# A rotary attention of 16 heads as one pipeline over four passes, with maxima ahead of copies on VectorE

## The chip, the cores and the metric

The kernel runs on 1 core of one Trainium2 chip. The metric is the device time of one execution in microseconds. The kernel before took 2139.44 us as the median of 3 runs (2137.86 to 2139.44).

## The reference

The reference is a chain of eight residual layers over 8 sequences of 256 tokens of width 128, all in fp32. Each layer adds `f(layernorm(x))` to `x`. The fifth is the layer that the change rewrites:

```
Q, K, V = x @ W_Q.T, x @ W_K.T, x @ W_V.T        # 16 heads of 8
Q, K = rope(Q), rope(K)                          # x * cos + flipped(x) * sin
scores = Q K^T / sqrt(8), causal mask
out = softmax(scores) V
return out.reshape(B, S, 128) @ W_O.T
```

Before it stand a linear attention, a feed-forward with 8 experts, a wide attention (16 heads of 64) and the same feed-forward; behind it a feed-forward with 32 experts, a state-space layer and that feed-forward again.

## The kernel before

The 2048 tokens are four passes of T = 512 (two sequences of L = 256). The residual `x` stays in SBUF, channels on partitions. The layers run one after another, each in a block of its own, which ends when all its engines have ended. Most layers are already one block over all four passes. The rotary attention is not: `attend` (L1939) calls `rotary_attention` (L325) once for each pass, so it is four blocks. Behind them `cut_weights` (L293) is a block that splits the up weights of the next layer into a high and a low part, ScalarE the high (L308) and VectorE the low (L314); these weights are loaded by a DMA issued just before the layer (L1931).

A pass has an edge at its start: the norm (L195 to L221: centre on TensorE, Square, mean, Ln and Exp on ScalarE, the product on VectorE), four projections into four banks (L369: query, its flipped form, key, its flipped form), the values (L371), 12 products that only keep TensorE running (L189), the rotation on VectorE (L473 to L475) and four copies of the key, each with all but one head in four set to zero (L477), so that one product over 32 rows gives the scores of one head. GpSimd clears the values' buffer (L440), and ScalarE lays the values into it (L448), 128 columns for each head of which 8 are not zero.

Then come 16 stages. A stage is (sequence b, head c within four, half jj): two heads m = 0, 1, each with 128 queries against 128 keys and 128 queries against 256 keys, that is 384 columns of scores. For a stage:
- TensorE: `scores(i)` (L385, L386) into banks 2(i%2) and 2(i%2)+1; `turn(i)`, six transposes of probabilities (L397) into banks 4 and 5; `weigh(i)`, the products with the values (L417, L419), which accumulate in bank 6. The order is scores(i+2), turn(i+1), weigh(i).
- VectorE: four operations (L491) that add the causal mask (`trib`), write the negated scores to SBUF and take the row minimum; then two copies of transposed probabilities (L501). In its round i it takes the minima of stage i and the copies of stage i-1.
- ScalarE: four exponentials in place with the sum of each row (L456).

scores(i) waits for the minima of stage i-2; turn(i) for the exponentials of stage i and for the copies of stage i-1; weigh(i) for the copies of stage i. Each pass ends with the reciprocals of the sums (L481, L482), their transposes (L405, L461), the product with them (L507), the output projection (L435) and the residual (L509).

Of the kernel before, what the change touches and what calls it, by code (L numbers as in the profile page):

```python
# [6 lines left out]
PASSES = 4  # L7
# [21 lines left out]
WARM = {"first": 4, "squares": 1, "norm": 6, "features": 10, "rotary": 12, "conv": 8, "parts": 24, "residual": 3}  # L29
# [12 lines left out]
def tables():  # L42

    const = layout([("mean", P), ("centre", P), ("ident", P), ("trib", 3 * P), ("cosq", L), ("sinq", L),
                    ("cosk", L), ("sink", L), ("keep", T), ("heads", P), ("hot", 2 * P), ("rows", 4), ("eps", 1),
                    ("seg0", NT * E0), ("seg1", NT * E1)])
    half = layout([("sel0", (E0 + 1) * P), ("sel1", (E1 // 2) * P), ("pick", 16 * P), ("lower", P), ("ones", P),
# [128 lines left out]
NORM = ["n_cent", "n_sq", "n_var", "n_ln", "n_rstd", "n_out"]  # L176

def halves():
    return [slice(b * L, (b + 1) * L) for b in range(NB)]  # L180

# [7 lines left out]

def norm_tensor(k, pe, s, p):

    for n, cols in enumerate(halves()):
        pe.matmul(k.bank[6 + n][:, 0:L], k.c("centre"), k.x[:, p, cols], start=True, stop=True).then_inc(s["n_cent"], 1)  # L195
    keep_clock(k, pe, WARM["squares"])
    for n, cols in enumerate(halves()):
        pe.wait_ge(s["n_sq"], n + 1)
        pe.matmul(k.bank[6 + n][:, L:2 * L], k.c("mean"), k.sq[:, cols], start=True, stop=True).then_inc(s["n_var"], 1)
    keep_clock(k, pe, WARM["norm"])  # L200
    pe.wait_ge(s["n_out"], NB)

def norm_scalar(k, act, s, then):

    for n, cols in enumerate(halves()):
        act.wait_ge(s["n_cent"], n + 1)
        act.activation(k.sq[:, cols], k.bank[6 + n][:, 0:L], ACT.Square).then_inc(s["n_sq"], 1)
    for n, cols in enumerate(halves()):
        act.wait_ge(s["n_var"], n + 1)  # L210
        act.activation(k.sq[:, cols], k.bank[6 + n][:, L:2 * L], ACT.Ln, bias=k.c("eps")).then_inc(s["n_ln"], 1)
        act.wait_ge(s["n_ln"], n + 1)
        act.activation(k.sq[:, cols], k.sq[:, cols], ACT.Exp, scale=-0.5).then_inc(s["n_rstd"], 1)
    if then is not None:
        act.preload_act_table_set(then)

def norm_vector(k, dve, s):
    for n, cols in enumerate(halves()):
        dve.wait_ge(s["n_rstd"], n + 1)  # L220
        dve.tensor_tensor(k.xn[:, 0, cols], k.bank[6 + n][:, 0:L], k.sq[:, cols], ALU.mult).then_inc(s["n_out"], 1)  # L221
    dve.wait_ge(s["n_out"], NB)
# [68 lines left out]

def cut_weights(k, n):  # L293

    nc = k.nc
    width, step = k.up_at[n][1], 4 * P
    cuts = [slice(at, at + step) for at in range(0, width, step)]
    s = k.semaphores(f"cut{n}", ["high"])
    with nc.Block(no_gpsimd_drain=True) as block:
        @block.sync  # L300
        def _(sp):
            k.zero_stale(sp, s)

        @block.scalar
        def _(act):
            act.wait_ge(k.up_loaded[n], 16)
            for cols in cuts:
                act.activation(k.up_high[n][:, cols], k.up_whole[n][:, cols], ACT.Copy).then_inc(s["high"], 1)  # L308

        @block.vector  # L310
        def _(dve):
            for i, cols in enumerate(cuts):
                dve.wait_ge(s["high"], i + 1)
                dve.tensor_tensor(k.up_low[n][:, cols], k.up_whole[n][:, cols], k.up_high[n][:, cols].bitcast(F32),  # L314
                                  ALU.subtract)

ATTEND = NORM + [
          "proj", "low", "high", "qk", "vcopy", "dve", "scores", "probs_in", "probs", "turned", "pt", "pv",
          "sums", "prod", "cleared", "k_turned", "k_tokens", "state", "states", "wide", "wide_t", "ot", "y",  # L320
          "done", "v", "v_act", "v_dve", "q", "qc", "q_low", "k", "kc", "k_low", "max", "pt_act", "pt_dve",
          "outn", "ot_act", "ot_dve"]

def rotary_attention(k, n, p):  # L325

    nc = k.nc
    G, layer, tag = 3, "rot", f"{n}p{p}"
    s = k.semaphores(f"attend{p % 2}", ATTEND)
    w = lambda name: k.w(G, name)
    stages = [(b, c, jj) for b in range(NB) for c in range(4) for jj in range(2)]
    NS = len(stages)
    with ExitStack() as ctx:  # L340
        def sb(name, shape, dt=F32):
            return ctx.enter_context(nc.sbuf_tensor(f"{layer}_{name}{tag}", shape, dt))
        vm = sb("v_by_head", [P, NT, H * (P + DA)])
        by_head = vm[:, :, 0:H * (P + DA)].rearrange("p t (h x) -> p t h x", x=P + DA)[:, :, :, 0:DA]
        q, kk = sb("q", [P, T]), sb("k", [P, T])
        km = sb("km", [P, 4, T])
        t1, t2 = sb("t1", [P, T]), sb("t2", [P, T])
        pin = sb("pin", [P, 2, 2, 3 * P])
        pt = sb("pt", [P, 2, 2, 3 * P])
        low = sb("low", [P, 2, 4])  # L350
        den = sb("den", [P, NT, H])
        wide = sb("wide", [P, NT, H, DA])
        ot = sb("ot", [P, T])
        block = ctx.enter_context(nc.Block(no_gpsimd_drain=True))

        @block.sync
        def _(sp):
            k.zero_stale(sp, s)

        @block.tensor  # L360
        def _(pe):
            pe.wait_ge(k.loaded, 16)
            pe.wait_ge(k.half_loaded, 16)
            pe.wait_ge(k.w_loaded[G], 16)
            norm_tensor(k, pe, s, p)

            names = ["wq", "wqf", "wk", "wkf"]
            for n, name in enumerate(names):
                pe.matmul(k.bank[n][:], w(name), k.xn[:, 0, :], start=True, stop=True).then_inc(s["proj"], 1)  # L369
            for j in range(NT):  # L370
                ins = pe.matmul(k.bank[4][:, j * P:(j + 1) * P], k.xn[:, 0, j * P:(j + 1) * P], w("wv"),  # L371
                                start=True, stop=True)
            ins.then_inc(s["proj"], 1)
            keep_clock(k, pe, WARM["rotary"])

            def scores(i):
                b, c, jj = stages[i]
                pe.wait_ge(s["qk"], c + 1)
                if i >= 2:
                    pe.wait_ge(s["probs_in"], i - 1)  # L380
                for m in range(2):
                    j = 2 * jj + m
                    r = slice(32 * j, 32 * j + 32)
                    t0, o = b * L, k.bank[2 * (i % 2) + m]
                    pe.matmul(o[:, 0:P], q[r, t0:t0 + P], km[r, c, t0:t0 + P], start=True, stop=True)  # L385
                    ins = pe.matmul(o[:, P:P + L], q[r, t0 + P:t0 + L], km[r, c, t0:t0 + L],  # L386
                                    start=True, stop=True)
                ins.then_inc(s["scores"], 1)

            def turn(i):  # L390

                pe.wait_ge(s["probs"], i + 1)
                if i >= 1:
                    pe.wait_ge(s["pt"], i)
                for m in range(2):
                    for n in range(3):
                        ins = pe.transpose(k.bank[4 + m][:, n * P:(n + 1) * P],  # L397
                                           pin[:, i % 2, m, n * P:(n + 1) * P], k.c("ident"))
                ins.then_inc(s["turned"], 1)

            def turn_shares():

                pe.wait_ge(s["wide"], 1)
                for j in range(NT):
                    ins = pe.transpose(k.bank[7][:, j * P:(j + 1) * P],  # L405
                                       wide[:, j].rearrange("p h e -> p (h e)"), k.c("ident"))
                ins.then_inc(s["wide_t"], 1)

            def weigh(i):

                b, c, jj = stages[i]
                pe.wait_ge(s["pt"], i + 1)
                for m in range(2):
                    head = 4 * (2 * jj + m) + c
                    p, first, last = pt[:, i % 2, m, :], c == jj == m == 0, head == 4 * 3 + 3
                    v = lambda tile: vm[:, tile, head * P:(head + 1) * P]
                    pe.matmul(k.bank[6][:, b * L:(b + 1) * L], v(2 * b), p[:, 0:L], start=first, stop=False,  # L417
                              skip_group_check=True)
                    ins = pe.matmul(k.bank[6][:, b * L + P:(b + 1) * L], v(2 * b + 1), p[:, L:L + P],  # L419
                                    start=False, stop=last, skip_group_check=True)  # L420
                ins.then_inc(s["pv"], 1)
# [1678 lines left out]
```

## Time and profile before

| what | us |
|---|---|
| median of 3 runs | 2139.44 (2137.86 to 2139.44) |
| profiled execution | 2135.41 |
| its span | 2133.6 |
| rotary attention, four passes | 879.0 to 1166.2 |
| cut of the next weights | 1166.2 to 1172.4 |
| busy over the whole span: PE, DVE, ACT, POOL | 1862.2, 1563.9, 879.9, 686.1 |
| mean granted TensorE clock | 0.968 |

### The profile page before, as it was taken

Reading aid. Unit: us, or ns where it says so; the run is one execution under the profiler, and the core shown is the slowest. Engines: PE = TensorE matmul, PEld = TensorE weight load, DVE = VectorE, ACT = ScalarE, POOL = GpSimd, SP = SyncE. Lnnn points to the kernel's source line nnn. Section 1 sums busy time; section 2 is a strip of 40 time slices with the busy share of each in tenths; the row PEclk is TensorE's granted clock in tenths of the full one; section 3 lists DMA queues with packets and bytes.
Section 4 is the critical chain, followed back from the end, with each engine's and each line's share of the span. In section 5 each row is a group of like instructions: output and inputs, shape, how many; then the busy total and the mean of one; then the engine's idle time right before and its main releaser. Section 6 shows DMA issues by size and latency. Waiting matters only on the chain. (4 is left out here: it accounts for less than half of the span.)

```text
span 2133.6 us, 23947 instructions
## 1 busy us (share of the span) xinstructions
PE 1862.2 (87%) x7515; PEld 996.0 (47%) x7527; DVE 1563.9 (73%) x2933; ACT 879.9 (41%) x2055; POOL 686.1 (32%) x757
## 2 busy tenths in 40 slices
PE   5779998999997999899888899968888878878998
PEld 2336653555553555567666455523232322225555
DVE  4868884555553788656556688749999999978887
ACT  2125544554543445345445333245444353332232
POOL 2642322433432222210110000027767677750000
PEclk8999999999999899999999899979999999999999
DMA  5000000000000000100000000000000000000000
GB/s 230 1 0 1 1 1 1 1 1 1 1 1 1 1 1 1 40 1 1 1 1 1 1 1 1 0 15 1 15 1 15 1 1 15 1 0 0 1 1 20
DMA packets 9628, 20.10 MB, mean 9 GB/s; under 512 B 1056, under 2 KB 8224, under 8 KB 8608
## 3 DMA queue, kind: packets, MB, share of 16 engines
q1 hardware_dynamic: 9504, 18.59, 2.6%
q8 instruction: 61, 1.00, 0.2%
q14 instruction: 63, 0.52, 0.1%
HBM read 14.39 MB, written 1.05 MB: 7 GB/s over the span
## 5 line engine op out<-in xcount | busy, mean ns | idle before, releaser
L1816 POOL TENSOR_TENSOR ssm_hc<-ssm_h,ssm_cm 128x512 f32<-128x512 f32 x256 | 334.3, 1308 | 135.3 <-DVE ssm_h L1899 135.0
L1899 DVE TENSOR_TENSOR_SCAN ssm_h<-banks,ssm_dbx 128x512 f32<-128x512 f32 x256 | 313.9, 1227 | 2.3 <-DVE ssm_dbx L1891 2.3
L515 PE MATMUL banks<-ffn_x_high,up_high 128*128 128x512 f32 x544 | 288.8, 531 | 6.0 <-ACT ffn_s1g L992 2.6
L1700 PE MATMUL banks<-ssm_hc,const 128*128 128x512 f32 x512 | 266.1, 601 | 12.2 <-DVE ssm_gated L1874 9.3
L1791 ACT ACTIVATE banks<-banks,a_neg 128x510 f32<-128x510 f32 x256 | 167.2, 659 | 242.6 <-PE banks L1687 241.6
L516 PE MATMUL banks<-ffn_x_low,up_high 128*128 128x512 f32 x544 | 218.3, 401 | 0.0
L517 PE MATMUL banks<-ffn_x_high,up_low 128*128 128x512 f32 x544 | 218.3, 401 | 0.0
L550 POOL TENSOR_TENSOR x_norm<-x_centred,x_square 128x512 f32<-128x512 f32 x28 | 37.9, 1354 | 492.5 <-ACT x_square L545 492.0
L1510 ACT ACTIVATE ffn_th<-banks 128x512 f32<-128x512 f32 (+1 forms) x136 | 81.2, 597 | 273.3 <-PE banks L517 224.6
L1891 DVE TENSOR_TENSOR ssm_dbx<-banks,ssm_bm 128x512 f32<-128x512 f32 x256 | 174.9, 683 | 19.3 <-PE banks L1690 18.8
L1325 POOL TENSOR_SCALAR wide_pin<-wide_pin,wide_rden 128x256 f32<-128x256 f32 x256 | 117.6, 478 | 217.0 <-DVE wide_rden L1349 217.0
L1687 PE MATMUL banks<-ssm_packed,half 96*128 96x510 bf16 x256 | 101.3, 396 | 73.2 <-DVE ssm_h L1899 66.1
L1460 PE MATMUL banks<-ffn_a,weights 128*128 128x512 f32 (+1 forms) x272 | 143.4, 608 | 22.6 <-DVE ffn_a L1550 21.8
L456 ACT ACTIVATE rot_pin4p<-rot_pin4p,rot_low4p 128x128 f32<-128x128 f32 (+1 forms) x256 | 113.1, 443 | 98.9 <-DVE rot_low4p L491 98.9
L1687 PEld LDWEIGHTS banks<-ssm_packed,half 96*128 96x128 bf16 x256 | 25.0, 98 | 261.3 <-DVE ssm_h L1899 235.7
L515 PEld LDWEIGHTS banks<-ffn_x_high,up_high 128*128 128x128 f32 x544 | 104.2, 192 | 86.3 <-issue 38.8
L1532 DVE SCALAR_TENSOR_TENSOR ffn_p<-ffn_th,banks 128x512 f32<-128x512 f32 (+1 forms) x136 | 93.2, 685 | 64.8 <-ACT ffn_th L1510 63.9
L516 PEld LDWEIGHTS banks<-ffn_x_low,up_high 128*128 128x128 f32 x544 | 104.7, 192 | 54.4 <-issue 38.9
L1700 PEld LDWEIGHTS banks<-ssm_hc,const 128*128 128x128 f32 x512 | 98.0, 193 | 56.1 <-POOL ssm_hc L1816 20.0
L1043 POOL TENSOR_SCALAR ffn_hg<-ffn_hg 128x512 f32<-128x512 f32 x72 | 44.2, 613 | 238.9 <-DVE ffn_hg L1063 238.9
L1302 ACT ACTIVATE wide_pin<-banks,wide_low 128x256 f32<-128x256 f32 x256 | 117.4, 477 | 8.0 <-DVE wide_low L1365 8.0
L491 DVE CUSTOM_DVE_ANT_0 rot_pin4p<-banks,const 128x128 f32<-128x128 f32 (+1 forms) x256 | 75.9, 354 | 58.5 <-PE banks L386 58.5
(245 smaller groups left out, 3623.5 us busy)
## 6 DMA issues: line engine op xcount, KB each, us to landing
ssm_packed<-ssm_parts SPq DMA_DIRECT2D x48, 64.0 KB, 2.0
up_whole<-in_up SPq DMA_DIRECT2D x1, 2304.0 KB, 16.2
weights<-in_weights SPq DMA_DIRECT2D x1, 2048.0 KB, 21.4
up_whole<-in_up SPq DMA_DIRECT2D x1, 2048.0 KB, 7.9
const<-in_const SPq DMA_DIRECT2D x1, 1426.5 KB, 6.2
half<-in_half SPq DMA_DIRECT2D x1, 1408.0 KB, 9.7
weights<-in_weights SPq DMA_DIRECT2D x1, 1168.0 KB, 23.9
weights<-in_weights SPq DMA_DIRECT2D x1, 1152.0 KB, 11.2
```

Of the source, the lines that this page charges most:

```text
L515: pe.matmul(out, w_high, x_high, start=True, stop=False)
L516: pe.matmul(out, w_high, x_low, start=False, stop=False)
L517: return pe.matmul(out, w_low, x_high, start=False, stop=True)
L1302: ins = act.activation(pin[:, i % RING, m, cols], k.bank[2 * (i % 2) + m][:, cols], ACT.Exp, bias=low[:, i % RING, n:n + 1], accum_out=den ...
L1325: ins = pool.tensor_scalar(part, part, rden[:, i % RING, n:n + 1], 1.0, ALU.mult, ALU.mult)
L1460: pe.matmul(k.bank[5][:], w("sd" if n == 0 else f"d{n - 1}")[0:rows, :], a[0:rows, g % 2, :], start=(n == 0), stop=(n == N - 1)).then_inc( ...
L1687: pe.matmul(two(k.bank[DELTA[i % AHEAD]])[:, :, 1:], pick, two(packed[0:96, p % 2, 0, g, :])[:, :, 1:], start=True, stop=True) \
L1700: pe.matmul(k.bank[5][:], k.c("hot")[:, P - row:2 * P - row], hc[:, i % HOLD, :], start=(i % NP == 0), stop=(i % NP == NP - 1)).then_inc(s ...
L1791: act.activation(spot_i, spot_i, ACT.Exp, scale=k.a_neg[:, i % NP:i % NP + 1]).then_inc(s["da"], 1)
L1816: pool.tensor_tensor(hc[:, i % HOLD, :], h[:, i % HOLD, :], cm[:, i // NP % 2, :], ALU.mult) \
L1891: dve.tensor_tensor(dbx[:, i % AHEAD, :], k.bank[DELTA_X[i % AHEAD]][:], bm[:, i // NP % 2, :], ALU.mult) \
L1899: dve.tensor_tensor_scan(h[:, n % HOLD, :], k.bank[DELTA[n % AHEAD]][:], dbx[:, n % AHEAD, :], 0.0, ALU.mult, ALU.add).then_inc(s["h"], 1)
```

## The change

`rotary_attention` becomes one block over the 64 stages of all four passes.

- The norm, the projections and the rotation of pass p+1 are issued within the stages of pass p (`ahead`, slots 6 to 13). All of them use bank 7. For pass 0 they run before the first stage.
- TensorE adds the causal mask: four bf16 products of `identb` with a new table `hide` (0 or -1e30), 128 columns each, behind the scores of a stage. The two heads' scores are issued in turns.
- VectorE takes maxima with two reductions over two banks at once, of 2 x 128 and 2 x 256 elements for each row. ScalarE reads the scores from PSUM and writes its exponentials to SBUF, into three buffers.
- The values take 32 columns for each head, so weighing puts the two heads into two column tiles of 32, in turns.
- The sums of the rotation, the four masked keys, the widening of the reciprocals and both parts of the cut of the next weights go to GpSimd, the cut as two of its eight pieces in each pass. The block `cut_weights` is gone, and with it `norm_tensor`, `norm_scalar`, `norm_vector`; `prepare_tensor`, `prepare_scalar`, `prepare_gpsimd` (L523 to L550, used by the other layers) take their place.
- The order on TensorE is scores(i), turn(i-2), weigh(i-3). In its round i VectorE takes the maxima of stage i and then the copies of stage i-3.

The core of the new function (p, b, c, jj = stage(i); NS = 16, ALL = 64, RING = DEEP = 3):

```diff
+        def _(pe):
+            def ahead(p, n):
+                ...
+                if n == 6:
+                    if p >= 1:
+                        pe.wait_ge(s["vm"], p)
+                    if p >= 2:
+                        pe.wait_ge(s["done"], p - 1)
+                    prepare_tensor(k, pe, s, p, 0)
+                if n == 7:
+                    prepare_tensor(k, pe, s, p, 1)
+                if 9 <= n < 13:
+                    c = n - 9
+                    pe.wait_ge(s["n_out"], p + 1)
+                    if c:
+                        pe.wait_ge(s["roped"], 4 * p + c)
+                    pe.matmul(k.bank[7][:], w(("wq", "wqf", "wk", "wkf")[c]), k.xn[:, p % 2, :], start=True, stop=True) \
+                        .then_inc(s["proj"], 1)
+                if n == 13:
+                    ...
+            def scores(i):
+                p, b, c, jj = stage(i)
+                if i % NS == 0:
+                    pe.wait_ge(s["q"], p + 1)
+                pe.wait_ge(s["km"], 4 * p + c + 1)
+                if i >= 2:
+                    pe.wait_ge(s["probs"], i - 1)
+                t0 = b * L
+                for t, (queries, keys) in enumerate(((slice(t0, t0 + P), slice(t0, t0 + P)),
+                                                     (slice(t0 + P, t0 + L), slice(t0, t0 + L)))):
+                    for m in range(2):
+                        r = slice(64 * jj + 32 * m, 64 * jj + 32 * m + 32)
+                        pe.matmul(k.bank[2 * (i % 2) + m][:, tiles[t]], q[r, p % 2, queries], km[r, p % 2, c, keys],
+                                  start=(t == 0), stop=False, skip_group_check=True)
+                for m in range(2):
+                    for first in (0, 2 * P):
+                        ins = pe.matmul(k.bank[2 * (i % 2) + m][:, first:first + P], k.h("identb"), k.h("hide"),
+                                        start=False, stop=True, skip_group_check=True)
+                ins.then_inc(s["scores"], 1)
+            def turn(i):
+                pe.wait_ge(s["probs"], i + 1)
+                if i >= 1:
+                    pe.wait_ge(s["pt"], i)
+                for m in range(2):
+                    for n in range(3):
+                        ins = pe.transpose(k.bank[4 + m][:, n * P:(n + 1) * P],
+                                           pin[:, i % RING, m, n * P:(n + 1) * P], k.c("ident"))
+                ins.then_inc(s["turned"], 1)
+            def weigh(i):
+                p, b, c, jj = stage(i)
+                pe.wait_ge(s["pt"], i + 1)
+                pe.wait_ge(s["vm"], p + 1)
+                if i % NS == 0 and p >= 1:
+                    pe.wait_ge(s["ot"], p)
+                for tile, (queries, part) in enumerate(((slice(b * L, (b + 1) * L), slice(0, L)),
+                                                        (slice(b * L + P, (b + 1) * L), slice(L, L + P)))):
+                    for m in range(2):
+                        j = 2 * jj + m
+                        ins = pe.matmul(k.bank[6][32 * j:32 * j + 32, queries], vm[:, p % 2, 2 * b + tile, 4 * j + c, :],
+                                        pt[:, i % 2, m, part], start=(c == tile == 0), stop=(c == 3 and tile == 1),
+                                        skip_group_check=True)
+                ins.then_inc(s["pv"], 1)
+            ...
+            for n in range(NS):
+                ahead(0, n)
+                if n in (6, 7, 12, 13):
+                    keep_clock(k, pe, WARM["first"])
+            for i in range(ALL + DEEP):
+                p, slot = i // NS, i % NS
+                if i < ALL:
+                    scores(i)
+                if slot == 2 and p >= 1:
+                    turn_shares(p - 1)
+                if slot == 4 and p >= 1:
+                    output(p - 1)
+                if i < ALL:
+                    ahead(p + 1, slot)
+                if 2 <= i < ALL + 2:
+                    turn(i - 2)
+                if i >= DEEP:
+                    weigh(i - DEEP)
+            output(PASSES - 1)
+            ...
+        def _(act):
+            ...
+            for i in range(ALL):
+                p, b, c, jj = stage(i)
+                act.wait_ge(s["max"], i + 1)
+                if i >= RING:
+                    act.wait_ge(s["turned"], i - RING + 1)
+                ...
+                        ins = act.activation(pin[:, i % RING, m, tiles[t]], k.bank[2 * (i % 2) + m][:, tiles[t]], ACT.Exp,
+                                             bias=low[:, i % RING, t, m:m + 1],
+                                             accum_out=den[:, p % 2, 2 * b + t, head:head + 1])
+                ins.then_inc(s["probs"], 1)
+                if i % NS == 2 and p >= 1:
+                    shared(p - 1)
+                ahead(p + 1, i % NS)
+            shared(PASSES - 1)
+        def _(pool):
+            pool.memset(vm[:], 0.0).then_inc(s["cleared"], 1)
+            pool.wait_ge(k.up_loaded[1], 16)
+            ...
+            for p in range(PASSES):
+                prepare_gpsimd(k, pool, s, p)
+                pool.wait_ge(s["roped"], 4 * p + 2)
+                pool.tensor_tensor(q[:, p % 2, :], t1[:], t2[:], ALU.add).then_inc(s["q"], 1)
+                pool.wait_ge(s["roped"], 4 * p + 4)
+                pool.tensor_tensor(kk[:], t1[:], t2[:], ALU.add).then_inc(s["k"], 1)
+                pool.wait_ge(s["k"], p + 1)
+                for c in range(4):
+                    pool.tensor_scalar(km[:, p % 2, c, :], kk[:], k.c("rows")[:, c:c + 1], 1.0, ALU.mult, ALU.mult) \
+                        .then_inc(s["km"], 1)
+                if p >= 1:
+                    widen(p - 1)
+                for i in (2 * p, 2 * p + 1):
+                    cols = cuts[i]
+                    pool.tensor_copy(k.up_high[1][:, cols], k.up_whole[1][:, cols]).then_inc(s["up_high"], 1)
+                    pool.wait_ge(s["up_high"], i + 1)
+                    pool.tensor_tensor(k.up_low[1][:, cols], k.up_whole[1][:, cols],
+                                       k.up_high[1][:, cols].bitcast(F32), ALU.subtract).then_inc(s["up_low"], 1)
+            widen(PASSES - 1)
+        def _(dve):
+            ...
+            for i in range(ALL + DEEP):
+                p, slot = i // NS, i % NS
+                if p >= 1 and slot == DEEP and i < ALL:
+                    normalise(p - 1)
+                if p >= 1 and slot == 5:
+                    residual(p - 1)
+                if i < ALL:
+                    dve.wait_ge(s["scores"], i + 1)
+                    for t in range(2):
+                        ins = dve.tensor_reduce(low[:, i % RING, t, :], k.banks[:, 2 * (i % 2):2 * (i % 2) + 2, tiles[t]],
+                                                AX_X, ALU.max, negate=True)
+                    ins.then_inc(s["max"], 1)
+                if i >= DEEP:
+                    n = i - DEEP
+                    dve.wait_ge(s["turned"], n + 1)
+                    if n >= 2:
+                        dve.wait_ge(s["pv"], n - 1)
+                    for m in range(2):
+                        ins = dve.tensor_copy(pt[:, n % 2, m, :], k.bank[4 + m][:, 0:3 * P])
+                    ins.then_inc(s["pt"], 1)
+                if p >= 1 and slot == 1:
+                    invert(p - 1)
+                if i < ALL:
+                    ahead(p + 1, slot)
+            normalise(PASSES - 1)
+            residual(PASSES - 1)
...
-                cut_weights(k, 1)
...
 PLAN = [linear_attention, biased_ffn, wide_attention, biased_ffn,
-        attend(rotary_attention), capped_ffn, state_space, capped_ffn]
+        rotary_attention, capped_ffn, state_space, capped_ffn]
```

`ahead` on VectorE (slots 9 to 12) multiplies one projection in bank 7 with its table, behind the copies of the round; on ScalarE it is the Square, Copy, Ln and Exp of the norm (slots 6 and 7) and four copies of values (slot 13).

## Rows read from the trace of the kernel before

**Rows 1.** Stretches: us; busy us of PE, PEld, DVE, ACT, POOL; clock; DMA; GB/s.
```profile
879.00:951.00 72.00, 63.50 (x403) 47.25 (x404) 43.22 (x176) 33.30 (x136) 7.35 (x2) 0.95 0.09 30
```

**Rows 2.** The page's costliest groups of instructions, the rotary stages.
```profile
L456 ACT ACTIVATE rot_pin4p<-rot_pin4p,rot_low4p 128x128 f32<-128x128 f32 (+1 forms) x256 | 113.1, 443 | 98.9 <-DVE rot_low4p L491 98.9
...
L491 DVE CUSTOM_DVE_ANT_0 rot_pin4p<-banks,const 128x128 f32<-128x128 f32 (+1 forms) x256 | 75.9, 354 | 58.5 <-PE banks L386 58.5
```

**Rows 3.** The timeline, steady stages: start us, us, instruction [idle before <-releaser].
```profile
907.91 0.50 PE L385 MATMUL banks<-rot_km4p,rot_q4p 32*128 32x128 f32 x4
...
908.78 0.87 PE L397 MATMUL banks<-const,rot_pin4p 128*128 128x128 f32 x6
...
908.90 0.29 DVE L491 CUSTOM_DVE_ANT_0 rot_pin4p<-banks,const 128x128 f32<-128x128 f32 x1 [1.14 <-PE banks L386]
...
909.49 0.60 PE L417 MATMUL banks<-rot_pt4p,rot_v_by_head4p 128*128 128x256 f32 x2
...
910.02 1.02 DVE L501 COPY rot_pt4p<-banks 128x384 f32<-128x384 f32 x2
...
910.89 0.50 PE L385 MATMUL banks<-rot_km4p,rot_q4p 32*128 32x128 f32 x4
...
914.17 0.50 PE L385 MATMUL banks<-rot_km4p,rot_q4p 32*128 32x128 f32 x4
```

**Rows 4.** The timeline, an early stage at the low clock.
```profile
896.20 0.81 PE L385 MATMUL banks<-rot_km4p,rot_q4p 32*128 32x128 f32 x4
...
897.79 1.54 PE L397 MATMUL banks<-const,rot_pin4p 128*128 128x128 f32 x6
...
897.92 0.29 DVE L491 CUSTOM_DVE_ANT_0 rot_pin4p<-banks,const 128x128 f32<-128x128 f32 x1 [0.58 <-PE banks L386]
...
899.12 1.06 PE L417 MATMUL banks<-rot_pt4p,rot_v_by_head4p 128*128 128x256 f32 x2
...
901.66 0.50 PE L385 MATMUL banks<-rot_km4p,rot_q4p 32*128 32x128 f32 x4
```

**Rows 5.** Groups by shape, and the timeline, for kinds of work that are added.
```profile
L1365 DVE TENSOR_REDUCE wide_low<-banks 128x4 f32<-128x1024 f32 x64 | 76.6, 1197 | 6.9 <-PE banks L1202 6.9
...
L619 DVE TENSOR_REDUCE ffn_r_top<-banks 128x4 f32<-128x128 f32 x8 | 2.3, 286 | 0.0
...
503.97 1.08 PE L1228 MATMUL banks<-wide_pt,wide_va 128*64 128x256 f32 x8
...
887.85 2.75 PE L189 MATMUL banks<-half 128*128 128x512 bf16 x12
```

**Rows 6.** The timeline at the stage's ends, groups on GpSimd, DMA issues.
```profile
883.42 3.70 PE L369 MATMUL banks<-x_norm,weights 128*128 128x512 f32 x8 [0.56 <-DVE x_norm L221]
...
885.52 0.69 DVE L473 TENSOR_TENSOR rot_t14p<-banks,const 128x512 f32<-128x512 f32 x1 [2.15 <-PE banks L369]
...
891.52 0.29 DVE L491 CUSTOM_DVE_ANT_0 rot_pin4p<-banks,const 128x128 f32<-128x128 f32 x1
...
1165.24 0.69 DVE L509 TENSOR_TENSOR x_resid<-x_resid,banks 128x512 f32<-128x512 f32 x1 [1.22 <-PE banks L435]
...
1172.40 2.05 PE L526 MATMUL banks<-x_resid,const 128*128 128x512 f32 x2 [6.55 <-PEq L299]
...
L550 POOL TENSOR_TENSOR x_norm<-x_centred,x_square 128x512 f32<-128x512 f32 x28 | 37.9, 1354 | 492.5 <-ACT x_square L545 492.0
...
up_whole<-in_up SPq DMA_DIRECT2D x1, 2048.0 KB, 7.9
```

**Rows 7.** The table of stretches, by granted clock.
```profile
655.66:669.31 13.65, 8.66 (x64) 5.40 (x64) 6.34 (x11) 6.72 (x26) 5.70 (x13) 1.00 0.00 1
669.31:672.73 3.42, 1.43 (x12) 1.12 (x14) 1.29 (x2) 0.00 (x0) 0.56 (x2) 1.00 0.00 0
672.73:679.56 6.83, 6.14 (x14) 2.52 (x11) 0.00 (x0) 0.60 (x1) 0.00 (x0) 0.50 0.00 0
...
1396.36:1410.01 13.65, 10.15 (x16) 2.89 (x14) 4.79 (x8) 7.03 (x9) 0.00 (x0) 0.50 0.01 1
```

More of the change, by code:

```diff
@@ L27 @@
 ALPHA, LIMIT = 1.702, 7.0
-WARM = {"first": 4, "squares": 1, "norm": 6, "features": 10, "rotary": 12, "conv": 8, "parts": 24, "residual": 3}
+WARM = {"first": 4, "features": 10, "parts": 24, "residual": 3}
 BIG = 1e30
@@ L189, in keep_clock @@
         pe.matmul(k.bank[bank][:], k.h("identb"), k.half[:, 0:512], start=True, stop=True)
[L192 to L222, printed above, removed]
 def turn_in(k, x_in):
@@ L290, in _ @@
                 dve.tensor_copy(tok[:, p].rearrange("p j d -> p (j d)"), k.bank[p][:]).then_inc(s["copied"], 1)
[L293 to L315, printed above, removed]
@@ L318 @@
[L318 to L421, printed above, removed]
-            scores(0)
-            scores(1)
-            pe.wait_ge(s["vcopy"], 1)
-            turn(0)
-            for i in range(NS):
-                if i + 2 < NS:
-                    scores(i + 2)
-                if i + 1 < NS:
-                    turn(i + 1)
-                weigh(i)
-            turn_shares()
-            pe.wait_ge(s["ot"], 1)
-            pe.matmul(k.bank[0][:], w("wo"), ot[:], start=True, stop=True).then_inc(s["y"], 1)
-            keep_clock(k, pe, WARM["residual"], bank=3)
-        @block.gpsimd
-        def _(pool):
-            pool.memset(vm[:], 0.0).then_inc(s["cleared"], 1)
-        @block.scalar
-        def _(act):
-            act.wait_ge(k.loaded, 16)
-            norm_scalar(k, act, s, None)
-            act.wait_ge(s["cleared"], 1)
-            act.wait_ge(s["proj"], 5)
-            act.activation(by_head, k.bank[4][:].rearrange("p (t h e) -> p t h e", t=NT, h=H),
-                           ACT.Copy).then_inc(s["vcopy"], 1)
-            for i in range(NS):
-                b, c, jj = stages[i]
-                act.wait_ge(s["probs_in"], i + 1)
-                for m in range(2):
-                    for t, cols in enumerate((slice(0, P), slice(P, 3 * P))):
-                        head = 4 * (2 * jj + m) + c
-                        ins = act.activation(pin[:, i % 2, m, cols], pin[:, i % 2, m, cols], ACT.Exp,
-                                             bias=low[:, i % 2, 2 * m + t:2 * m + t + 1], scale=-1.0,
-                                             accum_out=den[:, 2 * b + t, head:head + 1])
-                ins.then_inc(s["probs"], 1)
-            act.wait_ge(s["wide_t"], 1)
-            act.activation(t2[:], k.bank[7][:], ACT.Copy).then_inc(s["wide_t"], 1)
-        @block.vector
-        def _(dve):
-            link = chained(dve, s["dve"])
-            dve.wait_ge(k.loaded, 16)
-            norm_vector(k, dve, s)
-            rope = [(q, 0, 1, "cosq", "sinq"), (kk, 2, 3, "cosk", "sink")]
-            for o, a, f, cos, sin in rope:
-                dve.wait_ge(s["proj"], f + 1)
-                table = lambda name: spread(k.c(name), [P, NB, L], 1)
-                two = lambda ap: ap.rearrange("p (b t) -> p b t", b=NB)
-                link(dve.tensor_tensor(two(t1[:]), two(k.bank[a][:]), table(cos), ALU.mult))
-                link(dve.tensor_tensor(two(t2[:]), two(k.bank[f][:]), table(sin), ALU.mult))
-                link(dve.tensor_tensor(o[:], t1[:], t2[:], ALU.add))
-            for c in range(4):
-                dve.tensor_scalar(km[:, c, :], kk[:], k.c("rows")[:, c:c + 1], None, ALU.mult).then_inc(s["qk"], 1)
-            def shares():
-                link(dve.reciprocal(den[:], den[:]))
-                dve.tensor_copy(wide[:], spread(den[:], [P, NT, H, DA], 3)).then_inc(s["wide"], 1)
-            for i in range(NS + 1):
-                if i < NS:
-                    dve.wait_ge(s["scores"], i + 1)
-                    if i >= 2:
-                        dve.wait_ge(s["turned"], i - 1)
-                    for m in range(2):
-                        for t, cols in enumerate((slice(0, P), slice(P, 3 * P))):
-                            ins = dve.tensor_tensor_reduce(
-                                pin[:, i % 2, m, cols], k.bank[2 * (i % 2) + m][:, cols],
-                                k.c("trib")[:, cols], 1.0, 3e38, ALU.add, ALU.min,
-                                low[:, i % 2, 2 * m + t:2 * m + t + 1])
-                    ins.then_inc(s["probs_in"], 1)
-                if i >= 1:
-                    dve.wait_ge(s["turned"], i)
-                    if i >= 3:
-                        dve.wait_ge(s["pv"], i - 2)
-                    for m in range(2):
-                        ins = dve.tensor_copy(pt[:, (i - 1) % 2, m, :], k.bank[4 + m][:, 0:3 * P])
-                    ins.then_inc(s["pt"], 1)
-            dve.wait_ge(s["probs"], NS)
-            shares()
-            dve.wait_ge(s["pv"], NS)
-            dve.wait_ge(s["wide_t"], 2)
-            dve.tensor_tensor(ot[:], k.bank[6][:], t2[:], ALU.mult).then_inc(s["ot"], 1)
-            dve.wait_ge(s["y"], 1)
-            dve.tensor_tensor(k.x[:, p, :], k.x[:, p, :], k.bank[0][:], ALU.add).then_inc(s["done"], 1)
@@ L1972 @@
     put(const, const_at[0], "ident", np.eye(P))
-    hide = np.where(tri.T, 0.0, BIG)
-    put(const, const_at[0], "trib", np.concatenate([hide, hide * 0, hide], 1))
     pair = (idx % DA) % (DA // 2)
@@ L2014 @@
     put(half, half_at[0], "lower", tri)
+    put(half, half_at[0], "hide", np.where(tri.T, 0.0, -BIG))
     put(half, half_at[0], "ones", 1.0)
```

131 lines of the change are left out of this document (120 added, 11 removed).

## The prediction

> **What bounds the kernel now.** I read the page first, then the table of stretches for the part that is rewritten. The rotary stage runs from 879.0 us to the start of the next stage's products at 1172.4 [rows 6]: 293.4 us of a span of 2133.6. It is four equal passes of 71.8 us and, at its end, 6.4 us for the cut of the next weights. In a pass TensorE is busy 63.5 of 72 us, VectorE 43, ScalarE 33 and GpSimd 7 [rows 1]. The costliest groups say where the idle time of the others lies: ScalarE waits 98.9 us for row minima, VectorE 58.5 us for scores [rows 2]. So TensorE is the nearest to its bound, and in the steady stages (a pass has 16) it goes score products, transposes, weighing with gaps of tenths: from 907.91 to 910.89 is one stage of 2.98 us, and the next takes 3.28 us, so 3.13 us each [rows 3]. The minima (908.90) start when the scores are there, and the copies (910.02) when the minima are done; TensorE has the scores of two stages ahead in hand, so nothing of this chain closes on itself.
> Beside the steady stages a pass has its edges: 12.5 us from its start to its first minimum at 891.52 [rows 6], and a tail. The first stages run at the low clock: products that take 2.98 us a stage later take 5.46 us between 896.20 and 901.66 [rows 4].
>
> **What goes.** The edges of four passes become one prologue and one tail, and the cut (about 6 us on ScalarE and VectorE) goes to GpSimd. The minimum with an added mask becomes one plain maximum over two banks; the mask goes to TensorE. Weighing puts two heads into two column tiles at once. By busy time this is a lighter stage: VectorE some 2 us for maxima and copies, TensorE 0.86 + 0.23 + 0.71 + 0.65 us, ScalarE four exponentials of 0.44 us [rows 2] or 1.8 us, each plus work for the next pass of under half a us per stage. If engines only had to be kept busy, a stage would take about 2.9 us.
>
> **What comes: a closed loop.** That is not how the waits are laid. In round i TensorE issues scores(i), then turn(i-2), then weigh(i-3). turn(i-2) needs banks 4 and 5 free, and waits for the copy of stage i-3. VectorE takes in round i the maxima of stage i first, for which it waits on scores(i), and only then the copy of stage i-3. So the copy, though its transposes have long been ready, stands behind the maxima; turn(i-2) and weigh(i-3) stand behind the copy; and scores(i+1) are queued behind both on TensorE. All of it is in series: scores(i), maxima(i), copy(i-3), turn(i-2), weigh(i-3), scores(i+1). One trip of it is one stage.
>
> Its price at the full clock:
> - scores to maxima. Now 0.99 us from the first product to the first minimum [rows 3]. Four mask products are added: a bf16 product of 512 columns takes 0.229 us in a row of 12 [rows 5], so 128 columns take 0.057, four 0.23; a change of tile shape costs 0.1 (an fp32 product of 512 columns takes two passes of 0.43 us [rows 6], so two heads of 256 + 128 columns stream for 1.30 of the 1.40 us from 909.49 to 910.89, [rows 3]). 1.32 us. The bound above is 1.5, if each product waits for a weight load of 0.1 us.
> - maxima. The reduce of 128 elements takes 0.286 us and that of 1024 takes 1.197 [rows 5], so 1.02 ns per element: 0.42 for 256 and 0.68 for 512. Each next one starts 0.08 early, as two copies of 0.55 take 1.02. 0.94 us.
> - copy, unchanged in shape: 1.02 us [rows 3], and 0.06 us to TensorE.
> - six transposes: 908.78 to 909.49, 0.71 us.
> - weighing. Now 909.49 to 910.89, 1.40 us with the change of shape; 1.30 is streaming. Column tiles in pairs do run together: eight passes of 256 columns take 1.08 us in the wide attention [rows 5], half of what they would take one after another. 0.65, and 0.2 for two changes of shape: 0.85 us. The bound above is 1.5, if pairs of 32 columns don't overlap.
> Sum: 1.32 + 0.94 + 1.02 + 0.06 + 0.71 + 0.85 = **4.90 us** a stage, against 3.13 now.
>
> On the changes of shape: the rows show 0.1 us for one. The Trainium skill, page TensorEngine Tiling (Array Packing), section Key Properties, says that changing the tiling mode drains the TensorE. By that rule the stage, which has three changes where it had two, would pay for one more; the trace has it at a tenth of a us, which is in the sum.
>
> **What is hidden.** Everything of the next pass is issued by TensorE after scores(i), that is while VectorE does maxima and copy (1.96 us): at most 1.1 us of products a slot. VectorE's rotations, residual and shares (0.69 us each, [rows 6]) fall where it waits for transposes, weighing and scores (some 2.9 us). ScalarE has 1.8 us of work in 4.9, so the Square, Copy, Ln, Exp and four value copies fit. GpSimd's share of a pass (three two-operand operations and two subtractions at 1.3 us [rows 6], and seven lighter operations below that, under 16 us) has 78 us. All are costed at nothing, and the closed loop is their cover; if the loop were broken they would cost 0.3 to 0.5 us a stage. The probabilities (1.8 us after the maxima) are needed two rounds later.
>
> **The clock.** At the low level all TensorE terms double. From the slow stage [rows 4]: scores to first minimum 1.72, with 0.55 for the mask 2.27; transposes 1.33; weighing 2.54 less the change, halved, and two changes: 1.42; VectorE as before, 1.96 + 0.06. Sum 7.04, call it **7.0 us**. Which level holds? In the loop TensorE has nothing to do for some 2 us in each stage. In the last stages of the wide attention it was busy 8.66 of 13.65 us and kept the full clock; when the scores ran out it was busy 1.43 of 3.42 us, and the 6.83 us after that were granted half [rows 7]. In the new loop it is busy 2.8 of 4.9 us as such rows count, which lies between, and in the rounds without work ahead the part around the gap looks like the second. Once low, it would be busy 4.8 of 7.0 us, and a stretch with 10.15 of 13.65 us busy ran at the low level throughout [rows 7]. So it should fall and rise. Between never and always I take half of the time at each level: 1 / (0.5/4.9 + 0.5/7.0) = **5.76 us** a stage.
>
> **The ends.** Prologue: the centring, squares and logarithm as now, 5 us; GpSimd waits for the up weights (issued at 878.2, landed 7.9 us later, [rows 6]) and normalises by 887.5; four projections and rotations go through one bank, each 0.85 to 1.7 + 0.2 + 0.75 us, to 896 or 898; key sum and first mask on GpSimd, 2 us; scores. The first maximum is at 900, against 891.52 now. The next three rounds, bound by the exponentials, take 6.5 us: 27.5 from 879.0 to the maxima of stage 3. Then 60 rounds, then three copies with transposes and weighing between them, 8.5 us, and share product, output, residual of 0.69 us and the block's end, 3.7 us [rows 6]. Fixed part 39.7 us.
> Sum: 39.7 + 60 x 5.76 = 385 us, against 293.4: **+92 us**. The profiled execution took 2135.4 us (span 2133.6) and would take 2227; the median of the runs lies 4 us above it, so I say 2231.
>
> **Rivals.**
> A, the clock stays full. For it: the wide attention kept its clock when it was busy 63% of a stretch [rows 7], and the loop is at 58% without its work ahead and above it with that. Then 39.7 + 60 x 4.9 = 334, +40 us: 2180. Chance 0.17.
> B, the clock is low nearly throughout. 39.7 + 60 x 7.0 = 460, +166 us: 2306. The rows for it: stretches three quarters busy that stayed low, and that score products use 32 rows and weighing 32 columns at a time. Chance 0.17. The Trainium skill, page TensorE: Matmul & The Clock Gate, Part 4 (PE-mode transpose), says that transposes don't count as busy in the same way for the clock. By that rule the clock would see 2.1 busy us of 4.9 and B is what happens, 2306; no row here tells it apart, since the stretch of the wide attention that fell had lost its scores and kept its transposes.
> C, faster: the loop isn't closed, because VectorE reaches its copy before TensorE needs it, or the change otherwise isn't in series as I read it. Its place is the wait for banks 4 and 5. It decides from a stage below (293.4 - 39.7) / 60 = 4.23 us; with the engines kept busy, 2.9 us, the sum is 39.7 + 174 = 214, -80 us: 2060. Against it: waits of the code, which leave no other order, and no row here makes one of the terms 0.67 us shorter. Chance 0.04.
> The forecast, mixed clock: 0.62.
>
> **How the numbers follow.** The time is the forecast's. The range goes from rival A to rival B, 2178 to 2306, and takes in the bounds of mask and weighing (0.2 and 0.65 us a stage, at 60 stages 12 and 39 us above the forecast). Within 0.2% (4 us, about what a measurement of this kernel can tell) there is next to nothing: it would need a stage of 4.2 us by chance, 0.01. Faster is C with its slower half left out, 0.04. Slower has the rest, 0.95.
>
> **What would show it.** In the trace of the changed kernel: stages of the rotary part 4.9 us apart or more; VectorE's copies starting right behind its maxima, not after a wait for transposes; TensorE's longest waits being those of transposes for copies (about 2 us, 60 times); VectorE waiting for the mask products of the scores, some 2.9 us a stage less its work ahead; ScalarE idle more than half of the time; granted clock between 0.6 and 0.9 for the part, with several falls in each pass; maxima of 0.42 and 0.68 us; weighing in 0.7 us. The forecast is wrong if copies start before maxima of the same round, if the part takes under 300 us, or if one level of the clock holds throughout, which gives A or B.

## The result, and the profile after

The changed kernel takes 2244.81 us (median of 4 runs, 2243.88 to 2248.45) against 2139.44 before: ratio 1.0501 (95% interval 1.0484 to 1.0517), 105 us slower. It was forecast at 2231 and within 2178 to 2306. The profiled execution took 2243.88 us with a span of 2242.0, 108.4 above the span before. The next layer's first product starts at 1283.26, where it was 1172.40 [rows 6]; so the rotary part with the cut takes 404.3 us instead of 293.4, +110.9, and the three layers behind it give back 2.5.

Three stretches of the part, in the columns of [rows 1]: the pipeline from the maxima of stage 3 to those of stage 63; a part of pass 0 with work ahead in six of its seven stages (slots 7 to 13); and the last pass from slot 2 on, which has no next pass to work for.

```profile
908.30:1269.86 361.56, 262.19 (x1638) 151.64 (x1638) 129.40 (x261) 113.01 (x507) 32.22 (x36) 0.74 0.00 1
...
935.52:970.09 34.57, 25.10 (x200) 14.36 (x199) 16.04 (x33) 13.89 (x62) 6.49 (x7) 1.00 0.00 1
...
1181.20:1269.86 88.66, 63.14 (x344) 36.30 (x342) 26.63 (x54) 22.81 (x105) 0.20 (x1) 0.60 0.00 0
```

VectorE and ScalarE do not have more to do: in 361.6 us VectorE works 129.4 and ScalarE 113.0, about a third of the time each, where in a pass before they worked 43.2 and 33.3 of 72 us [rows 1]. Yet a stage takes 6.03 us in the mean, where one of the steady part before took 3.13. The time is in waits. From the list of waits of the same pipeline (us in total, times, longest):

```profile
ACT rot_pin L1050 <- DVE rot_low L1136: 245.1, 60, 5.5
DVE rot_low L1136 <- PE banks L945: 220.8, 60, 5.2
...
PE banks L956 <- DVE rot_pt L1145: 99.4, 60, 2.1
```

Each occurs 60 times, once a stage: maxima wait for the mask products, exponentials for maxima, and transposes (L956) for the copies (L1145). Before, the third did not exist. One stage at the full clock, in the timeline, answers to [rows 3]:

```profile
940.46 1.02 DVE L1136 TENSOR_REDUCE rot_low<-banks 128x2 f32<-128x256 f32 x2 [2.99 <-PE banks L945]
941.39 1.01 DVE L1145 COPY rot_pt<-banks 128x384 f32<-128x384 f32 x2
...
942.55 0.84 PE L956 MATMUL banks<-const,rot_pin 128*128 128x128 f32 x6 [2.13 <-DVE rot_pt L1145]
...
943.33 0.84 PE L971 MATMUL banks<-rot_pt,rot_v_by_head 128*32 128x256 f32 x8
944.10 0.92 PE L941 MATMUL banks<-rot_km,rot_q 32*128 32x128 f32 x8
944.96 0.40 PE L945 MATMUL banks<-half 128*128 128x128 bf16 x4
...
945.39 1.02 DVE L1136 TENSOR_REDUCE rot_low<-banks 128x2 f32<-128x256 f32 x2 [2.99 <-PE banks L945]
```

Read it as a ring: maxima, copies, transposes, weighing, scores, mask, maxima. Twice in a trip one engine releases the other: the copies release TensorE's transposes, and the mask products release VectorE's maxima. What lies between follows in each engine's order of issue, without a wait, and the trip takes 4.94 us. The same at the low clock answers to [rows 4] and takes 7.19 us:

```profile
1187.90 1.02 DVE L1136 TENSOR_REDUCE rot_low<-banks 128x2 f32<-128x256 f32 x2 [1.42 <-PE banks L945]
1188.84 1.01 DVE L1145 COPY rot_pt<-banks 128x384 f32<-128x384 f32 x2
...
1190.00 1.51 PE L956 MATMUL banks<-const,rot_pin 128*128 128x128 f32 x6 [2.13 <-DVE rot_pt L1145]
...
1191.44 1.50 PE L971 MATMUL banks<-rot_pt,rot_v_by_head 128*32 128x256 f32 x8
1192.87 1.65 PE L941 MATMUL banks<-rot_km,rot_q 32*128 32x128 f32 x8
...
1195.09 1.02 DVE L1136 TENSOR_REDUCE rot_low<-banks 128x2 f32<-128x256 f32 x2 [5.24 <-PE banks L945]
```

### The profile page after: what moved, and what is told of

Its sections match the earlier page's. It is cut to its first block and busy times, and to the rows that moved or that the text cites. A ratio compares the mean times of both kernels' runs of the same rounds, so it can differ in the third digit from the quotient of the medians.

```text
span 2242.0 us, 23945 instructions
## 1 busy us (share of the span) xinstructions
PE 1900.3 (85%) x7698; PEld 976.0 (44%) x7698; DVE 1527.3 (68%) x2505; ACT 865.8 (39%) x2051; POOL 702.9 (31%) x802
## 5 line engine op out<-in xcount | busy, mean ns | idle before, releaser
L1740 PE MATMUL banks<-ssm_hc,const 128*128 128x512 f32 x512 | 266.9, 603 | 12.2 <-DVE ssm_gated L1914 9.3
L1136 DVE TENSOR_REDUCE rot_low<-banks 128x2 f32<-128x256 f32 (+1 forms) x128 | 65.4, 552 | 232.0 <-PE banks L945 232.0
L291 POOL TENSOR_TENSOR x_norm<-x_centred,x_square 128x512 f32<-128x512 f32 x32 | 42.9, 1340 | 528.3 <-ACT x_square L286 524.3
L1050 ACT ACTIVATE rot_pin<-banks,rot_low 128x128 f32<-128x128 f32 (+1 forms) x256 | 104.0, 419 | 253.7 <-DVE rot_low L1136 253.7
L956 PE MATMUL banks<-const,rot_pin 128*128 128x128 f32 x384 | 73.1, 342 | 101.8 <-DVE rot_pt L1145 101.8
## 6 DMA issues: line engine op xcount, KB each, us to landing
weights<-in_weights SPq DMA_DIRECT2D x1, 1168.0 KB, 23.9
```

The costliest lines, as they stand in the source:

```text
L1740: pe.matmul(k.bank[5][:], k.c("hot")[:, P - row:2 * P - row], hc[:, i % HOLD, :], start=(i % NP == 0), stop=(i % NP == NP - 1)).then_inc(s ...
```

## The experiments

**First, the loop with its clock held.** The kernel `e2_fill_gap` adds products that nobody reads. They stand in each round in which TensorE has no other work beside the stages, 37 of the 64. The code is abridged:

```diff
                 if i < ALL:
                     ahead(p + 1, slot)
+                    fill(p, slot)      # in free slots: keep_clock(k, pe, 4, bank=7), behind bank 7's last reader
                 if 2 <= i < ALL + 2:
                     turn(i - 2)
```

> The changed kernel, with four bf16 products of 512 columns that nobody reads put on TensorE between scores(i) and turn(i-2), in every slot that has no work ahead. Closed loop with the clock on top of it (my theory): the products (about 0.9 us) lie in TensorE's 2.1 us of waiting, so they cost nothing, and the clock stays full: every stage takes 4.94 us instead of a mean of 6.03, 60 x 1.09 = 65 us less than the changed kernel, about 2180 us. Rival, the slow stages have another cause than the clock (GpSimd's work, waits on bank 7): the stages without work ahead stay at 6.5 to 7.2 us, about 2245 or more.

Measured: 2180.92 us (2175.61 to 2185.05), ratio to the kernel before 1.0197 (1.0178 to 1.0216). The stretch of its pipeline:

```profile
907.00:1203.33 296.33, 218.95 (x1749) 125.34 (x1770) 129.50 (x261) 113.34 (x508) 32.30 (x36) 1.00 0.00 1
```

In a plain stage of its timeline the products (L182) lie in the gap, and the transposes still wait for the copies behind them, 1.27 us instead of 2.13:

```profile
966.06 1.03 PE L182 MATMUL banks<-half 128*128 128x512 bf16 x4
968.36 0.85 PE L956 MATMUL banks<-const,rot_pin 128*128 128x128 f32 x6 [1.27 <-DVE rot_pt L1165]
```

60 stages take 296.3 us, 4.94 each, all at the full clock. So more work on TensorE made the kernel 64 us faster. Two things follow: what a stage took beyond 4.94 us was the clock's, and 0.9 us of products in a gap cost nothing in the loop.

**Then each side of the loop, on that kernel.** Three edits, each alone: the four mask products left out (the scores are then not masked, so the attention isn't causal); one more reduction on VectorE between maxima and copies; the same one behind the copies. The code is abridged.

```diff
-                for m in range(2):                        # e4_fill_no_mask
-                    for first in (0, 2 * P):
-                        ins = pe.matmul(..., k.h("identb"), k.h("hide"), ...)
...
                     ins.then_inc(s["max"], 1)
+                if i < ALL:                               # e5_fill_extra_between
+                    dve.tensor_reduce(spare[:, i, :], k.const[:, 0:256] as 2 x 128, AX_X, ALU.max)
                 if i >= DEEP:
...
                     ins.then_inc(s["pt"], 1)
+                if i < ALL:                               # e6_fill_extra_behind
+                    dve.tensor_reduce(spare[:, i, :], k.const[:, 0:256] as 2 x 128, AX_X, ALU.max)
```

> As the filled kernel, without the four mask products of a stage (the scores are not masked, so the attention isn't causal). Closed loop: whatever is between the scores and the maxima is paid in full, 0.25 to 0.33 us a stage, 16 to 21 us in 64 stages: about 2161 us if the filled kernel takes 2180. Rival, TensorE has slack in each stage, as it idles for 2 us: no difference.

> As the filled kernel, with one reduction of 256 SBUF elements a row, which nobody reads, on VectorE between the maxima and the copies. Closed loop: paid in full, 0.34 us a stage, +22 us in 64 stages: about 2202 us. Rival, VectorE is under half busy and hides it: no difference.

> As the filled kernel, with the same reduction behind the copies of a round, where VectorE waits for scores for some 3 us. Closed loop: hidden, within 2 us of the filled kernel. Rival, VectorE's total work sets the stage: +22 us, as in the kernel that has it between.

| on the filled kernel | median us | against 2180.92 | a stage at the full clock |
|---|---|---|---|
| no mask products | 2163.51 (2161.61 to 2164.25) | -17.4 | 4.62 |
| reduction between | 2204.77 (2201.84 to 2208.96) | +23.9 | 5.27 |
| reduction behind | 2182.98 (2179.43 to 2186.79) | +2.1 | 4.94 |

The stages are the distances of successive maxima in the traces, where nearly all of them are equal. From the maxima of stage 3 to those of stage 63 the filled kernel took 296.3 us, and the three edits 280.8, 319.5 and 298.0. That is 60 times the difference of a stage, and 3.6, 3.5 and 1.6 us for three, two and one stages in which the clock fell after all. Without the mask products, a stage is 0.32 us shorter, although TensorE idles in each. With 0.33 us more on VectorE it is 0.33 us longer or no longer at all, by where the work stands. The two places in the timelines, first between, then behind:

```profile
1164.03 1.02 DVE L1157 TENSOR_REDUCE rot_low<-banks 128x2 f32<-128x256 f32 x2 [0.48 <-PE banks L946]
1164.97 0.41 DVE L1161 TENSOR_REDUCE rot_spare<-const 128x2 f32<-128x256 f32 x1
1165.30 1.01 DVE L1168 COPY rot_pt<-banks 128x384 f32<-128x384 f32 x2
```

```profile
1162.79 1.02 DVE L1157 TENSOR_REDUCE rot_low<-banks 128x2 f32<-128x256 f32 x2 [2.07 <-PE banks L946]
1163.73 1.01 DVE L1166 COPY rot_pt<-banks 128x384 f32<-128x384 f32 x2
1164.66 0.41 DVE L1169 TENSOR_REDUCE rot_spare<-const 128x2 f32<-128x256 f32 x1
```

The reduction of 0.41 us overlaps the next by 0.08, so it moves the copies by 0.33.

**Then the loop opened, from either side,** on the changed kernel without filling. One edit exchanges VectorE's two halves of a round, the other leaves them and issues the scores earlier on TensorE:

```diff
+                if i >= DEEP:                             # e1_copies_first: copies of stage i-3 first
+                    ...
                 if i < ALL:
                     dve.wait_ge(s["scores"], i + 1)
                     ...
-                if i >= DEEP:
-                    ...
```

```diff
+            scores(0)                                     # e3_scores_early
             for i in range(ALL + DEEP):
                 p, slot = i // NS, i % NS
-                if i < ALL:
-                    scores(i)
+                if i + 1 < ALL:
+                    scores(i + 1)
```

> The changed kernel with one edit: in its round VectorE takes the copies of stage i-3 first and the maxima of stage i second. Closed loop: copy(i-3) no longer waits for scores(i), so a trip of the loop goes over two rounds and TensorE becomes the bound, 1.09 + 0.78 + 0.77 us of scores with mask, transposes and weighing and 0.4 us of work ahead, about 3.0 us a stage; 60 x (6.03 - 3.0) = 180 us less than the changed kernel, about 2065 us, faster than the kernel before. Rival, the loss is the clock's alone: then the swap brings the full clock at best, 4.94 us a stage, 2180 us.

> The changed kernel with VectorE's order left as it is (maxima first) and the loop opened on TensorE: scores(i+1) are issued in round i, ahead of turn(i-2). Closed loop: maxima(i) find their scores done a round earlier, so this opens it as well: about 3.0 us a stage, about 2065 us. Rival, it is VectorE's order as such that costs: then it stays near 2245 us.

> Both edits: copies first and scores a round early. Closed loop: one edit is enough, TensorE stays the bound, so the same as the better of the two within 10 us. Rival, each edit takes away a different part of the wait: the two together gain clearly more than either.

| kernel | median us | ratio to before (95%) |
|---|---|---|
| copies first | 2084.07 (2079.91 to 2090.51) | 0.9746 (0.9726 to 0.9765) |
| scores early | 2080.35 (2069.58 to 2083.78) | 0.9709 (0.9682 to 0.9736) |
| both | 2085.62 (2079.80 to 2092.24) | 0.9751 (0.9729 to 0.9774) |

Either edit turns 5% slower into 2.5 to 3% faster, and both together give no more than one. A plain stage of the kernel with copies first, on TensorE:

```profile
948.94 0.82 PE L956 MATMUL banks<-const,rot_pin 128*128 128x128 f32 x6
949.70 0.84 PE L971 MATMUL banks<-rot_pt,rot_v_by_head 128*32 128x256 f32 x8
950.47 0.92 PE L941 MATMUL banks<-rot_km,rot_q 32*128 32x128 f32 x8
951.33 0.40 PE L945 MATMUL banks<-half 128*128 128x128 bf16 x4
951.56 0.82 PE L956 MATMUL banks<-const,rot_pin 128*128 128x128 f32 x6
```

TensorE waits for nothing there; a stage is 2.62 us, and TensorE is the bound. The expected 3.0 us a stage was too low as a mean: the traces have 3.30 with copies first and 3.18 with early scores, so the kernels came 19 and 15 us above the expected 2065. With both edits it is 3.34, since another wait appears: in every second plain stage the scores wait for the exponentials of two stages before, and that stage takes 3.18 us.

```profile
1091.53 0.92 PE L941 MATMUL banks<-rot_km,rot_q 32*128 32x128 f32 x8 [0.49 <-ACT rot_pin L1051]
```

What is hidden in the closed loop lies bare in the open one. Rounds with work ahead take 3.53 us (2.62 + 0.91), and between slots 2 and 6 the shares product and the residual stand on VectorE ahead of the maxima and wait. That gave a last edit, on the kernel with early scores: the two put behind the maxima of their round. The kernel with early scores ran again beside it, as `e3_again`.

```diff
-                if p >= 1 and slot == DEEP and i < ALL:
-                    normalise(p - 1)
-                if p >= 1 and slot == 5:
-                    residual(p - 1)
                 if i < ALL:
                     ...
                     ins.then_inc(s["max"], 1)
+                if p >= 1 and slot == DEEP and i < ALL:
+                    normalise(p - 1)
+                if p >= 1 and slot == 5:
+                    residual(p - 1)
```

> The kernel with scores a round early, and the shares product (slot 3) and the residual (slot 5) put behind the maxima of their round instead of ahead of them. With the loop open, work that was hidden in it lies on the path: in the trace of the kernel with early scores the maxima of slot 3 stand 2.5 us behind the shares product's wait, and those of slot 5 some 1.9 us behind the residual's. If that is what those rounds lose, three passes gain up to 13 us: about 2068 to 2072 us. Rival, TensorE is the bound there as well and its products of those slots only move: within 3 us of the kernel with early scores, 2080 us.

> The kernel with scores a round early, unchanged, beside it on the same chip: 2080 us as before, to compare the other with.

Measured: 2073.03 us (2068.66 to 2074.46), ratio 0.9690 (0.9677 to 0.9703); beside it early scores alone 2082.35 us (2069.25 to 2083.80), ratio 0.9724 (0.9698 to 0.9749). This is the lowest median, 3.1% under the kernel before. But the two intervals touch, and it isn't shown that the kernel with the edit is faster than the one without: the runs of early scores fall into two groups, near 2069.4 and near 2082, and the lower one is as fast as this. The difference of the groups is for the most part not the attention's: of the 14.2 us between a trace of each (spans 2067.7 and 2081.9), 9.3 lie in the layers before and behind it, whose code is the same. The timelines around slot 3, first early scores alone, then with the edit:

```profile
955.22 1.02 DVE L1137 TENSOR_REDUCE rot_low<-banks 128x2 f32<-128x256 f32 x2 [0.21 <-PE banks L945]
956.15 1.01 DVE L1146 COPY rot_pt<-banks 128x384 f32<-128x384 f32 x2
959.72 0.69 DVE L1120 TENSOR_TENSOR rot_ot<-banks,rot_shares 128x512 f32<-128x512 f32 x1 [2.55 <-PE banks L971]
960.33 1.01 DVE L1137 TENSOR_REDUCE rot_low<-banks 128x2 f32<-128x256 f32 x2
```

```profile
963.00 1.02 DVE L1133 TENSOR_REDUCE rot_low<-banks 128x2 f32<-128x256 f32 x2 [0.67 <-PE banks L945]
964.88 0.69 DVE L1120 TENSOR_TENSOR rot_ot<-banks,rot_shares 128x512 f32<-128x512 f32 x1 [0.86 <-PE banks L971]
```

The wait of 2.55 us before the shares product shrinks to 0.86. From the maxima of slot 2 to those of slot 7 it is 955.22 to 971.70 in the one, and 960.38 to 975.63 in the other: 16.48 and 15.25 us, so 1.2 us a pass and 3.7 in three. That is all that the traces show for the edit. The expected 13 took each wait for a loss; most of them only moved TensorE's products of those slots, as the rival had it. That the median of 2073.03 lies so near the expected 2068 to 2072 is luck.

## Why the prediction was right

**The closed loop** is what happened, and it is shown from six sides: the 60 waits of transposes for copies, the two prices paid in full, the one hidden, and the two openings. Term by term at the full clock, predicted and measured: scores with mask to maxima 1.32 and 1.29 us; maxima 0.94 and 0.93; copies to the first transpose 1.08 and 1.16; transposes 0.71 and 0.78; weighing 0.85 and 0.77. Sum 4.90 and 4.94. At the low clock 7.0 and 7.19. TensorE's terms did not double there, as the prediction put it before it took them from [rows 4]: transposes went from 0.78 to 1.44 us, weighing from 0.77 to 1.43, and all of them together from 2.84 to 5.09. The split of the part before doesn't quite add up either: four passes of 71.8 us leave 6.2 us for the cut, not 6.4; the sum uses only the total.

**Small bounds.** The mask costs 0.32 us in the run without it, against 0.33 in the sum (0.23 and a change of shape of 0.1). The timeline of the kernel with copies first has 0.23 us from the first mask product to the next transposes, which leaves 0.09 us for the change of shape; no run measures it by itself. The Trainium skill, page TensorEngine Tiling (Array Packing), section Key Properties, says that changing the tiling mode drains TensorE. The 0.09 us are what the runs leave for one such change. The pairs of 32-column tiles run together: weighing takes 0.77 us from its start to the next scores, where the same columns took 1.40 before [rows 3].

**The clock** was the open term. I took half of the time at each level, a choice between never and always that no row fixed; that it came out near was luck. The mean stage was 6.03 us against 5.76, so 60 x (6.03 - 5.76) = 16 us more than forecast, the one large miss. The share itself was nearly right: the granted clock was low in 190 of the pipeline's 361.6 us, 53%. The formula 1 / ((1 - x)/4.94 + x/7.19) gives only 5.91 us for that, because it takes every microsecond at the low level alike. In the trace the low level held for 62% of the time from the start of the transposes to the next maxima, where TensorE is the one that works on the loop, and for 35% of the time of maxima and copies, where its clock costs nothing. So of the 16 us some 6 are the sizes of the two stages, 3 the share, and 7 where the low stretches fell.

The mean hides a pattern that I had only touched on with "rounds without work ahead". In slots 9 to 13 of a pass with work ahead, where products for the next pass fill the gap, no fall begins. It falls in slot 14 each time and is mostly low until slot 4 or so, in pass 0 until slot 6. In passes 1 and 2 it also falls once in slot 8, which has no work ahead on TensorE, for 6.8 us. The last pass from slot 2 on, with nothing ahead, has a mean granted clock of 0.60. Rival A (full throughout) is what the filled kernel does, 2180.92 us against its 2180. Rival B (low throughout, 2306) did not come: the clock rose again and again, even between the stages of 7.19 us of the last pass. The Trainium skill, page TensorE: Matmul & The Clock Gate, Part 4 (PE-mode transpose), says that transposes don't count as busy in the same way for the clock. No run here tells whether they do; only the consequence that the prediction drew from it, rival B, did not come.

**The ends.** From the start to the maxima of stage 3 29.3 us against 27.5, from those of stage 63 to the next layer 13.4 against 12.2; the first maximum came at 900.35, forecast 900. That is 3 us, and with the 16 of the clock 19 of the part's 404.3 against 385; the three layers behind gave 2.5 back, and the median lies 0.9 us above the profiled execution and not 4, which leaves the 14 between 2245 and 2231. Rival C, faster, asked for a stage under 4.23 us; the code's waits excluded it, and it is what the kernels with the loop opened are. Everything costed at nothing was hidden: in the filled kernel the slots with the rotation, the residual and the norm of the next pass take 4.94 us like the empty ones.

## What to carry to other kernels

When two engines exchange several results a round, write each engine's order of issue down and follow the waits around: if a trip returns in the same round, the stage is the sum of its members, however idle the engines are, and every instruction on it costs its full time. Moving one link a round earlier, on either engine, makes the trip span two rounds; here it gave the busiest engine back as the bound in the plain stages, 2.62 us instead of 4.94. Open the loop on one side and then read the waits anew, for moving both links brought another wait. A loop that idles TensorE can be paid a second time in its clock: here 0.9 us of useless products in the gap cost nothing and gave back 64 us.

## What was not expected

It was not expected that so little work decides on the clock. The filled kernel adds 0.9 us of products in 37 of the 64 stages and is 64 us faster (2244.81 to 2180.92 us), its pipeline at 2.4 GHz from end to end. And in the changed kernel's trace all 17 falls between the maxima of stage 3 and those of stage 63 begin in rounds whose gap has no 512-column product in it; none begins in a round that has one.
